# Taking the exponential of attention scores on the way out of PSUM, in two attention layers on one core

## What is computed

```
x = x + attn_a(layernorm(x))     # 16 heads of 8, softmax inside blocks of 64 positions
x = x + moe(layernorm(x))        # 8 experts, top 2, hidden 512
x = x + attn_b(layernorm(x))     # 16 heads of 8, attention along the 16 rows, bias on neighbours
x = x + moe(layernorm(x))
```

```
scores = q . k * scale (+ bias)
attn   = exp(scores - max(scores)) / sum(exp(scores - max(scores)))
out    = attn . v
```

## Time and profile before

| what | us |
|---|---|
| time, median of 3 runs | 886.98 (883.74 to 887.29) |
| span of the profiled execution | 926.2 |
| first layer, in that span | 24 to 258 |
| experts a | 258 to 472 |
| second layer | 472 to 688 |
| experts b | 688 to 898 |
| combine | 898 to 926 |

### The profile page before, as it was taken

How to read it: one execution, slowest core, us unless ns; L and a number is a source line. 1 busy time by engine, 2 the same in 40 slices (tenths; PEclk the granted TensorE clock), 3 DMA queues, 4 the chain that set the end, 5 groups by cost and what they waited for, 6 DMA issues and landing times. The chain is left out here.

```text
span 926.2 us, 27043 instructions
## 1 busy us (share of the span) xinstructions
PE 746.1 (81%) x8818; PEld 600.2 (65%) x8819; DVE 505.9 (55%) x1787; ACT 524.2 (57%) x1016; POOL 363.0 (39%) x446
## 2 busy tenths in 40 slices
PE   1688887786179999999967898877629999999970
PEld 1356655455158888888834677666518888888860
DVE  3366876653435555555527565454435555555534
ACT  0589975652056666666617986643116666666630
POOL 0454764536713333333333114447642333333330
PEclk9989987885589999999999997997659999999985
DMA  6134011011211111111135000111121111111117
GB/s 193 38 98 121 22 40 36 25 31 56 75 39 48 46 46 46 49 49 46 38 107 172 11 4 24 30 33 41 40 72 40 48 49 47 46 46 46 49 33 268
DMA packets 53546, 54.45 MB, mean 59 GB/s; under 512 B 8192, under 2 KB 43008, under 8 KB 53472
## 3 DMA queue, kind: packets, MB, share of 16 engines
q1 hardware_dynamic: 41024, 31.61, 12.2%
q0 software_dynamic: 8640, 18.11, 6.0%
q10 hardware_dynamic: 3808, 3.70, 1.2%
HBM read 29.51 MB, written 23.86 MB: 58 GB/s over the span
## 5 line engine op out<-in xcount | busy, mean ns | idle before, releaser
L1656 POOL DMA_INDIRECT expert_out<-moe_b_out,moe_b_place x71 | 68.0, 957 | 145.3 <-DVE moe_b_out L1812 145.3
L1656 POOL DMA_INDIRECT expert_out<-moe_a_out,moe_a_place x71 | 68.0, 958 | 145.1 <-DVE moe_a_out L1812 145.1
L1688 PE MATMUL wide<-wgu,moe_b_hi 128*128 x284 | 94.9, 415 | 0.0
L1688 PE MATMUL wide<-wgu,moe_a_hi 128*128 x284 | 94.3, 413 | 0.0
L1069 POOL DMA_INDIRECT routed<-stream,lb_place x64 | 62.3, 974 | 63.1 <-PE wide L1117 18.5
L479 POOL DMA_INDIRECT routed<-stream,la_place x64 | 63.2, 987 | 42.9 <-DVE la_place L784 26.2
L1704 PE MATMUL wide<-wd,moe_a_hidT 128*128 x568 | 75.5, 276 | 1.4 <-DVE moe_a_out L1812 0.7
L1704 PE MATMUL wide<-wd,moe_b_hidT 128*128 x568 | 75.4, 276 | 1.3 <-DVE moe_b_out L1812 0.7
L1704 PEld LDWEIGHTS wide<-wd,moe_b_hidT 128*128 128x128 f32 x568 | 69.0, 192 | 2.2 <-issue 2.2
L1704 PEld LDWEIGHTS wide<-wd,moe_a_hidT 128*128 128x128 f32 x568 | 69.0, 192 | 2.2 <-issue 2.0
L1763 ACT ACTIVATE moe_b_glow<-wide 128x512 f32<-128x512 f32 x71 | 42.6, 599 | 44.1 <-PE wide L1688 44.0
(11 more groups left out here) (282 smaller groups left out, 1778.3 us busy)
## 6 DMA issues: line engine op xcount, KB each, us to landing
moe_a_rows<-routed SPq DMA_DIRECT2D x71, 67.0 KB
moe_b_rows<-routed SPq DMA_DIRECT2D x71, 67.0 KB
lb_outs<-expert_out SPq DMA_DIRECT2D x8, 512.0 KB
la_stage<-in_wg SPq DMA_DIRECT2D x8, 256.0 KB, 2.6
la_stage<-in_wu SPq DMA_DIRECT2D x8, 256.0 KB, 3.2
wd<-in_wd SPq DMA_DIRECT2D x8, 256.0 KB, 3.8
kept<-stream SPq DMA_DIRECT2D x8, 256.0 KB
lb_kept<-kept SPq DMA_DIRECT2D x8, 256.0 KB
```

The source lines that it names most:

```text
L1656: pool.indirect_dma_start(d.expert[:, :], bass.IndirectOffsetOnAxis(ap=place[s % 4][:, 0:1], axis=0), out[u][:, :], None).then_inc(stored[ ...
L1688: last = nc.tensor.matmul(ps[u][:, :], x[u][:, :], w(j, part), start=i == 0, stop=i == 2)
```

## The change

The exponential in SBUF goes, in both layers. The copy out of PSUM behind the transposes becomes the exponential. `turn` waits for `shifted` in place of `risen`, and all waits on `flat_copied` become waits on `risen`, which is now counted by the exponential out of PSUM with the same numbers. The order of everything else stays.

```diff
@@ first_layer, TensorE
             def turn(p, gp, w):
                 unit = 4 * p + 2 * gp + w
-                pe.wait_ge(risen, 2 * p + gp + 1)
+                pe.wait_ge(shifted, 2 * p + gp + 1)
                 if unit >= 2:
-                    pe.wait_ge(flat_copied, unit - 1)
+                    pe.wait_ge(risen, unit - 1)
@@ first_layer, ScalarE
-            def rise_up(p, gp):
-                act.wait_ge(shifted, 2 * p + gp + 1)
-                nc.scalar.activation(prob[p % 2][:, gp, :], prob[p % 2][:, gp, :], ACT.Exp).then_inc(risen, 1)
-
-            def out_flat(p, gp, w):
+            def rise_up(p, gp, w):
                 act.wait_ge(flat, 4 * p + 2 * gp + w + 1)
                 if p >= 2 and gp == 0 and w == 0:
                     act.wait_ge(mixed, p - 1)
-                nc.scalar.activation(probT[p % 2][gp][w][:, :], psP[w], ACT.Copy).then_inc(flat_copied, 1)
+                nc.scalar.activation(probT[p % 2][gp][w][:, :], psP[w], ACT.Exp).then_inc(risen, 1)
@@ first_layer, ScalarE's order
-                if here:
-                    rise_up(p, 0)
...
                 if here:
-                    out_flat(p, 0, 0)
-                    out_flat(p, 0, 1)
-                    rise_up(p, 1)
+                    rise_up(p, 0, 0)
+                    rise_up(p, 0, 1)
...
                 if here:
-                    out_flat(p, 1, 0)
-                    out_flat(p, 1, 1)
+                    rise_up(p, 1, 0)
+                    rise_up(p, 1, 1)
@@ second_layer, ScalarE
-                nc.scalar.activation(probT(c, gp, w)[:, :], psP[w], ACT.Copy).then_inc(flat_copied, 1)
+                nc.scalar.activation(probT(c, gp, w)[:, :], psP[w], ACT.Exp).then_inc(risen, 1)
```

More of the change, by code:

```diff
@@ L343, in first_layer @@
         "k_out", "v_ready", "v_out")
-    scored, peaked, shifted, risen, flat, flat_copied, mixed, mixed_copied, flipped, inverted, divided, based, summed = counted(
-        k, tag, "scored", "peaked", "shifted", "risen", "flat", "flat_copied", "mixed", "mixed_copied", "flipped",
+    scored, peaked, shifted, flat, risen, mixed, mixed_copied, flipped, inverted, divided, based, summed = counted(
+        k, tag, "scored", "peaked", "shifted", "flat", "risen", "mixed", "mixed_copied", "flipped",
         "inverted", "divided", "based", "summed")
@@ L511, in turn_x @@
                 if c >= 2:
-                    pe.wait_ge(flat_copied, 8 * (c - 2) + 7)
+                    pe.wait_ge(risen, 8 * (c - 2) + 7)
                 for t in range(BATCH):
@@ L543, in turn_x2 @@
                 pe.wait_ge(summed, 2 * c + 2)
-                pe.wait_ge(flat_copied, min(8 * (c + 2) + 3, 4 * PAIRS))
+                pe.wait_ge(risen, min(8 * (c + 2) + 3, 4 * PAIRS))
                 for t in range(BATCH):
@@ L613, in mixing @@
                 c = p // 2
-                pe.wait_ge(flat_copied, 4 * p + 4)
+                pe.wait_ge(risen, 4 * p + 4)
                 pe.wait_ge(v_out, c + 1)
@@ L950, in second_layer @@
         "k_out", "v_ready", "v_out")
-    scored, peaked, shifted, risen, flat, flat_copied, mixed, mixed_copied, flipped, inverted, divided = counted(
-        k, tag, "scored", "peaked", "shifted", "risen", "flat", "flat_copied", "mixed", "mixed_copied", "flipped",
+    scored, peaked, shifted, flat, risen, mixed, mixed_copied, flipped, inverted, divided = counted(
+        k, tag, "scored", "peaked", "shifted", "flat", "risen", "mixed", "mixed_copied", "flipped",
         "inverted", "divided")
@@ L1099, in turn_x @@
                 if c >= 3:
-                    pe.wait_ge(flat_copied, 4 * (c - 3) + 3)
+                    pe.wait_ge(risen, 4 * (c - 3) + 3)
                 elif c >= 1:
@@ L1133, in turn_x2 @@
                 if c == 0:
-                    pe.wait_ge(flat_copied, 10)
+                    pe.wait_ge(risen, 10)
                 else:
@@ L1142, in route_logits @@
                 pe.wait_ge(copied2, c + 1)
-                pe.wait_ge(flat_copied, min(4 * (c + 2) + 4, 4 * QUADS))
+                pe.wait_ge(risen, min(4 * (c + 2) + 4, 4 * QUADS))
                 for t in range(BATCH):
@@ L1152, in route_ranks @@
                 pe.wait_ge(picked, c + 1)
-                pe.wait_ge(flat_copied, min(4 * (c + 3) + 2, 4 * QUADS))
+                pe.wait_ge(risen, min(4 * (c + 3) + 2, 4 * QUADS))
                 out = psP[1][:, 0:BATCH * EXPERTS].rearrange("p (t e) -> p t e", e=EXPERTS)
@@ L1187, in turn @@
             def turn(c, gp, w):
-                pe.wait_ge(risen, 2 * c + gp + 1)
+                pe.wait_ge(shifted, 2 * c + gp + 1)
                 if gp == 0 and w == 0:
@@ L1193, in turn @@
                     else:
-                        pe.wait_ge(flat_copied, 4 * c - 1)
+                        pe.wait_ge(risen, 4 * c - 1)
                 elif gp == 0:
@@ L1198, in turn @@
                     elif c >= 1:
-                        pe.wait_ge(flat_copied, 4 * c)
+                        pe.wait_ge(risen, 4 * c)
                 elif w == 0:
@@ L1203, in turn @@
                     else:
-                        pe.wait_ge(flat_copied, 4 * c + 1)
+                        pe.wait_ge(risen, 4 * c + 1)
                 elif c >= 2:
@@ L1207, in turn @@
                 else:
-                    pe.wait_ge(flat_copied, 4 * c + 2)
+                    pe.wait_ge(risen, 4 * c + 2)
                 for i in range(4):
@@ L1216, in mixing @@
                 o = 2 * c + w
-                pe.wait_ge(flat_copied, 4 * c + 4)
+                pe.wait_ge(risen, 4 * c + 4)
                 pe.wait_ge(v_out, c + 1)
@@ L1240, in turn_back @@
                 pe.wait_ge(divided, 2 * c + 2)
-                pe.wait_ge(flat_copied, min(4 * (c + 2) + 1, 4 * QUADS))
+                pe.wait_ge(risen, min(4 * (c + 2) + 1, 4 * QUADS))
                 if c == QUADS - 1:
@@ L1543, in out_back, with rise_up @@
                 nc.scalar.activation(mixT[:, :], psP[0], ACT.Copy).then_inc(back_copied, 1)
[L1545 to L1549, removed]
+            def rise_up(c, gp, w):
                 act.wait_ge(flat, 4 * c + 2 * gp + w + 1)
@@ L1569, in _ @@
             for c in range(-3, QUADS + 3):
-                if 0 <= c < QUADS:
-                    rise_up(c, 0)
                 if 0 <= c + 2 < QUADS:
@@ L1575, in _ @@
                     out_v(c)
-                    out_flat(c, 0, 0)
-                    out_flat(c, 0, 1)
+                    rise_up(c, 0, 0)
+                    rise_up(c, 0, 1)
                 if 0 <= c - 1 < QUADS:
@@ L1583, in _ @@
                     out_back(c - 2)
-                if 0 <= c < QUADS:
-                    rise_up(c, 1)
                 if 0 <= c + 2 < QUADS:
@@ L1594, in _ @@
                 if 0 <= c < QUADS:
-                    out_flat(c, 1, 0)
+                    rise_up(c, 1, 0)
                 if 0 <= c + 2 < QUADS:
@@ L1598, in _ @@
                 if 0 <= c < QUADS:
-                    out_flat(c, 1, 1)
+                    rise_up(c, 1, 1)
             act.wait_ge(table_sem, 1)
```

## The result

| kernel | median us | runs | ratio to before, 95% interval |
|---|---|---|---|
| before | 885.36 (877.74 to 887.29) | 4 | |
| after | 876.50 (872.66 to 881.46) | 4 | 0.9898 (0.9858 to 0.9938) |
| after, second measurement on another occasion | 875.12 (before: 885.12) | 12 | 0.9882 (0.9849 to 0.9915) |

The change makes the kernel some 9 to 10 us faster. The forecast was 876.0 us.

The account below looks back on a forecast made before the run. ScalarE was taken as the fuller engine only at each layer's start, TensorE close behind, so only TensorE's idle waits were priced: 8.1 + 3.0 = 11.1 us off 886.98, giving 876 us, range 863 to 885.

Parts of the forecast that it names:

- Rival 1: Whole kernel: TensorE is the bound, ScalarE's relief is idle time; only 0.94 + 0.64 us go, 885.4 us; chance 0.14.
- The moved wait at nothing: Transposes of both layers now wait for VectorE's subtraction, claimed always done by then, so no cost.
- The first layer, 8.1 us: First attention layer: TensorE's waits that go, 6.5 + 0.94 + 0.64 = 8.1 us.
- Quads 2 and 3 of the signs: Second and third quad of the first layer, expected in the profile after with periods of 16.6 and 18.8 us.
- The waits of L608 (6.5 us): First layer: transposes' waits for the SBUF exponential go, 4.9 us in full plus 1.6 of 2.2 put down to "issue".
- the 0.64: First layer, second quad: the transpose back (L633) waits 0.64 us for a side copy behind an exponential; all goes.
- the 1.60: First layer, first quad: TensorE waits 1.60 us before the query projection for the key copy; 0.94 us of it goes.
- The second layer, 3.0 us: Second attention layer: gain of 0.94 + 0.54 + 1.5 = 3.0 us.
- 0.94 goes, 0.54 goes: Second layer: 0.94 of TensorE's 1.19 us key-copy wait at 511.50 and its 0.54 us full-queue wait at 513.60 disappear.
- The 0.3 us for each of five late quads: Second layer, last five quads from 536.74 on: an estimated 0.3 us each of TensorE's 0.66 us idle, 1.5 in all.
- rival 2: Both layers: three half-clock stretches of TensorE, 3.4 us each, go with their waits; 866 us; chance 0.20.
- rival 3: Both layers: bunched pauses before L514 and L546 lower TensorE's clock, 3.4 us each; slower, 888 to 900; chance 0.06.

Follow-up runs that it names:

- the idle pass: Changed kernel with a 128x1024 exponential of unread data at each old place in ScalarE's queue, transposes not waiting for it; 933.79 us, ratio 0.9937 to the kernel before.
- The pair on one chip: Changed kernel, second measurement, 875.12 us, beside the changed kernel with an unread exponential put back that the transposes wait for, 884.77 us.
- the waited pass: Changed kernel with an unread 128x1024 exponential at each old place and TensorE's transposes waiting for it; 884.77 us, ratio 0.9999 to the kernel before.

## Why the prediction was right, and where it was not

**What bounds the layers: right.** The cut by quads told what the whole-span shares did not. Rival 1, TensorE as the bound and a gain of 1.6 us, is out: 0.9898 and 0.9882 both exclude 885.4 us. The share of 81% said little about the first layer, where ScalarE was the fuller. Two of its parts hold: after the change TensorE is fuller than ScalarE there, with VectorE as full in some quads, and a wait that goes while ScalarE stays full does come back at the copies, as the idle pass showed. The Trainium skill, Perfetto Trace Analysis, section Optimization Strategy, says that the most-contended engine can change over time; here it changed both along the kernel and with the edit.

**Cost of the exponential out of PSUM: right.** Taken as 598 ns, measured 598 and 595.

**ScalarE's busy time: over-stated.** I wrote 51 us less and measured 43.9. The sum of 48 durations counts overlaps that a union counts once; my own 0.94 us each, 45 us, was the number to give.

**The moved wait at nothing: right, nearly.** No wait of TensorE in L608 or L1204 for the subtraction is in the list of waits after, only the short ones of their weight loads. What the prediction left out is that the next scores come to wait for the subtraction, 2.2 us in 3 places.

**The first layer, 8.1 us: right in sum, and in most terms.** Quads 2 and 3 of the signs, 16.6 and 18.8 us, measured 16.45 and 18.70. The waits of L608 (6.5 us) are gone, the 0.64 too, and the 1.60 became 0.98, so 0.62 went where I had counted 0.94. The pair on one chip gives 8.6 to 9.8 us for the layer. Its six quads lose 1.74, 1.74, 0.90, 1.39, 0.86 and 0.73 us where the sum has 1.73, 1.43 and then 0.79 each. The pause of 1.04 before L514 stayed, at 1.07, as said. What was wrong is the reason for "in full". I asked only whether the transposes could start, and not what the copies behind the pass then delay. With the wait gone and ScalarE still full, two quads got back 0.28 us each and not 0.79. The waits went in full because the queue was freed with them, and the sum does not say so. The first quad of the earlier trace rows, 20.15 to 16.44 us, gained more than its waits: the waited pass has 18.19 there at full clock, so some 2 us of the 3.7 go with the stretch at half clock.

**The second layer, 3.0 us: wrong.** The runs gave 1.000. The step that failed is "0.94 goes, 0.54 goes". I read that the key copy stood behind an exponential and took the whole delay of the copy for a gain of the wait. Its wait shrank from 1.19 to 1.00. The step "goes" for 0.54 named a full queue, but the copy that ended it stood behind key copies and `lb_norm`, and the wait stayed. The 0.3 us for each of five late quads was an estimate without a wait under it, and the row at 506.84 has 15.47 after 15.50. The 0.66 us that one early quad did gain at full clock was in none of the terms. The question I had not asked is what is late next once the copy starts earlier.

**The clock (rivals 2 and 3): both in small.** The stretch at half clock in the first quad of the earlier trace rows is in none of the five traces whose first layer has the change without a pass put back. It is in seven of the nine others, the idle pass among them, where the 0.79 us wait was gone and the one for the key copy, 1.63 us, was not. The other two had the low clock up to about 46 us instead, as told above. So that much of rival 2 came true. The layer got other stretches instead: the quad at 94.97 has a granted clock of 0.92 and lasts 20.68 us, while the same quad of the same kernel had 1.00 and 19.23 us on another occasion. Such a stretch costs about 1.4 us there, and three of them in one execution stayed far from the price of rival 3. The Trainium skill, TensorE: Matmul & The Clock Gate, section A second HAM failure mode: psum-queue depth-cycling, describes a clock that swings as TensorE pauses between groups. The trace agrees for the first quad, where the clock fell behind the longer pause only (1.16 to 1.63 us, against 0.98 or less). For the second layer it is open: with the three pauses of one quad filled the next still fell, and nothing that was measured was saved.

**The level of the profile: wrong, without harm.** I expected a span of 915 us and it was 874.2. I took the 39 us between span and median for something that only a profile has. They were the distance between two levels of execution, and the forecast gain held at either level: 0.9904 for the first layer alone where before takes 937 us, 0.9882 for all where it takes 885.

## What to carry to other kernels

Cut the span down to the loop's own period before asking which engine bounds it, and price an edit by the waits that end on the removed instruction, not by its busy time: 45 us of queue were worth 9. Then ask whether the engine stays full without the wait: if it does, the wait comes back at its next copy (0.28 us of 1.72 were gained so). For each wait that goes, look up what its releaser itself stood behind and what is late next; in the second layer the wait for the key copy stayed at 1.00 of 1.19 us though ScalarE got idle time. When a trace's span differs from the median by more than a few us, ask whether it is another level of execution, and take the terms from quads that look the same in both.

## What the runs showed of the hardware

The same kernel before took 885 us on two occasions and 934 and 937 us on two others, each run within 1.5% of its median. Waits of TensorE in mixing, first in the 926.2 us trace of the kernel before, then in the 888.8 us trace of the kernel before with the moved value copies, which leaves this line alone:

```profile
PE wide L1227 <- issue: 15.8, 28, 1.4
```

```profile
PE wide L1227 <- issue: 3.6, 4, 1.7
```

On the slower level TensorE stops inside a run of matmuls that wait for nothing that the profile shows, 28 times in place of 4. It is so in all fourteen traces: 23 to 32 such stops in the nine with a span over 900 us, 4 in the five under 900. ScalarE's waits with releaser "remote" are in all of the nine and in none of the five. Both fit instructions or signals of TensorE that arrive late. What makes them late was not tested.

Not expected either: filling pauses ahead of a fall of the clock did not prevent it. It came one quad later, after a quad with 94% of TensorE busy (10.69 of 11.32 us).

In the first layer the fall follows one pause. TensorE waits for the key copy before the query projection (L527, the 1.60 us of the earlier trace rows). In the seven traces where this wait was 1.16 to 1.63 us a stretch at half clock follows it; in the seven where it was 0.98 us or less none does. The rows don't tell whether the length of the pause or something that goes with it decides.
